# x loaded two batches ahead, gate rows issued behind the maxima, and the maxima turned earlier and sent from ScalarE

## What is computed

```
mod = silu(c) @ wmod                                   # per batch: shifts, scales and gates
h   = layernorm(x) * (1 + ca) + sa
q, k, v = h @ w_dq.T @ w_uq.T, split(h @ w_dkv.T @ w_ukv.T)   # 16 heads of 16 features
x   = x + ga * (softmax(causal(q @ k.T / 4)) @ v @ w_out.T)
h   = layernorm(x) * (1 + cb) + sb
x   = x + gb * (out0 where expert 0 has the larger logit, else out1)
      out0 = gelu(h @ W0a.T + b0a) @ W0b.T + b0b,  out1 = relu(h @ W1a.T + b1a) @ W1b.T + b1b
```

## Time and profile before

| | |
|---|---|
| median of 3 runs | 679.35 us (678.64 to 680.35) |
| the profiled execution | 680.1 us, of which the span from first to last instruction 678.3 us |
| PE busy | 560.5 us (83% of the span) |
| DVE, ACT, POOL busy | 440.7, 367.0, 267.7 us |
| mean granted TensorE clock | 0.872 of full speed |
| transfers | 43.87 MB, mean 65 GB/s |

### The profile page before, as it was taken

One profiled execution on the slowest core, in us unless ns is written; L12 is line 12 of the kernel. 1 busy time (PEld: TensorE's weight loads), 2 busy tenths in 40 slices (PEclk: granted clock), 3 DMA queues, 4 the chain that ended last, 5 costly groups with the idle time before them and its releaser, 6 DMA issues.

```text
span 678.3 us, 14114 instructions
## 1 busy us (share of the span) xinstructions
PE 560.5 (83%) x4912; PEld 472.4 (70%) x4912; DVE 440.7 (65%) x885; ACT 367.0 (54%) x521; POOL 267.7 (39%) x268
## 2 busy tenths in 40 slices
PE   5353939899797979798897979797997979799984
PEld 4242627688686868687786868686876768778874
DVE  2463436388584949586785949495876859397463
ACT  2333625747483847467473838476474748384520
POOL 3140304245252535445442525344452525253351
PEclk9755575989797989989797979899897979799997
DMA  8806070705325170807153260808062331601100
GB/s 274 151 10 95 1 128 1 125 3 77 67 51 93 23 122 2 141 0 112 29 69 73 41 101 9 132 0 138 3 88 54 57 89 32 96 1 34 33 17 15
DMA packets 43562, 43.87 MB, mean 65 GB/s; under 512 B 5360, under 2 KB 40560, under 8 KB 43520
## 3 DMA queue, kind: packets, MB, share of 16 engines
q1 hardware_dynamic: 43520, 43.33, 36.6%
HBM read 13.39 MB, written 4.23 MB: 26 GB/s over the span
## 4 chain that ended last, share of the span: by engine, by line
PE 58%; DMA 17%; SPq 14%; issue 5%; DVE 4%; ACT 2%; POOL 0%; POOLq 0%; DVEq 0%; ACTq 0%
DMA qs<-mx_rows 14%; SPq L286 11%; PE ps_t L410 7%; PE ps_t L414 6%; PE ps_s L389 6%; PE ps_o L338 4%; PE ps_c L338 4%; PE ps_o L339 4%; PE ps_o L340 4%; PE ps_c L339 3%; PE ps_c L340 3%; PE ps_a L338 3%; PE ps_a L340 3%; PE ps_a L339 2%; PE ps_o L428 2%
## 5 line engine op out<-in xcount | busy, mean ns | idle before, releaser
L803 ACT ACTIVATE score_rows<-ps_s 128x1024 f32<-128x1024 f32 x96 | 98.8, 1030 | 92.7 <-PE ps_s L389 76.6
L816 ACT ACTIVATE p<-ps_t 128x1024 f32<-128x1024 f32 x96 | 98.2, 1023 | 70.7 <-PE ps_t L414 69.8
L1225 POOL TENSOR_SCALAR_AFFINE_SELECT score_rows<-score_rows 128x512 f32<-128x512 f32 (+1 forms) x96 | 85.2, 888 | 114.8 <-ACT score_rows L803 114.7
L943 DVE TENSOR_REDUCE mx<-score_rows 128x4 f32<-128x1024 f32 (+1 forms) x96 | 115.0, 1211 | 11.0 <-POOL score_rows L1225 11.0
L410 PE MATMUL ps_t<-qs,ks 50*128 50x256 f32 (+1 forms) x512 | 60.2, 342 | 73.0 <-DMA qs<-mx_rows 72.3
L410 PEld LDWEIGHTS ps_t<-qs,ks 50*128 50x128 f32 x512 | 44.6, 229 | 82.5 <-DMA qs<-mx_rows 49.4
L389 PE MATMUL ps_s<-ks,qs 48*128 48x256 f32 (+1 forms) x512 | 58.4, 331 | 16.4 <-DMA ks<-parts_k 14.0
L866 DVE BATCH_NORM_STATS2 ln_st<-xs 128x6 f32<-128x256 f32 (+1 forms) x64 | 23.9, 414 | 73.7 <-DMA xs<-x 69.8
L1177 POOL TENSOR_TENSOR xs<-z,xs 128x512 f32<-128x512 f32 (+1 forms) x16 | 27.7, 1733 | 104.3 <-DVE z L1015 104.3
L1168 POOL TENSOR_TENSOR ln_rs<-ln_ve,neg_half 128x2 f32<-128x2 f32 x32 | 24.1, 755 | 108.7 <-DVE ln_ve L872 108.7
L389 PEld LDWEIGHTS ps_s<-ks,qs 48*128 48x128 f32 x512 | 39.8, 205 | 34.8 <-issue 21.4
(11 more groups left out here) (160 smaller groups left out, 1650.5 us busy)
## 6 DMA issues: line engine op xcount, KB each, us to landing
qs<-parts_q SPq DMA_DIRECT2D x96, 128.0 KB, 4.3
ks<-parts_k SPq DMA_DIRECT2D x96, 128.0 KB, 5.8
xs<-x SPq DMA_DIRECT2D x16, 256.0 KB, 6.7
gates<-gates_scratch SPq DMA_DIRECT2D x16, 256.0 KB, 6.1
out<-xs SPq DMA_DIRECT2D x16, 256.0 KB, 5.6
p<-wmod SPq DMA_DIRECT2D x1, 1024.0 KB, 6.2
p<-waT SPq DMA_DIRECT2D x1, 1024.0 KB, 8.3
p<-wmod SPq DMA_DIRECT2D x1, 512.0 KB, 5.9
```

The lines of the kernel that those rows point to most:

```text
L803: act.activation(score_rows[c % 2][:], ps_s[:], ACT.Copy).then_inc(scores_out, 1)
L816: act.activation(by_side, ps_t[:].rearrange("p (k h s) -> p k h s", k=2, h=n // 2), ACT.Exp, scale=SCALE).then_inc(exp_done, 1)
L943: dve.tensor_reduce(dst, score_rows[c % 2][:].rearrange("p (k h s) -> p k h s", k=2, h=n), AX_X, ALU.max).then_inc(max_done, 1)
L1225: pool.affine_select(out=diag, in_=diag, compare_op=ALU.is_ge, fill=NEG, base=0, pattern=[[0, n], [-1, P]], channel_multiplier=1).then_inc ...
```

## The change

Four things are changed. The maxima are turned in the bank of the keys (`ps_b`), and one step earlier in the listing: `turn_maxima(at(1), ...)` stands before the last `up` group of the step rather than `turn_maxima(at(2), ...)` at the head of the next. ACT itself issues the two transfers of the maxima, behind a wait for its own copy, and `maxima_rows` stands before `values_copy` instead of behind it. SP no longer issues the maxima. And SP loads x two batches ahead, as the last transfer of its step. The lists of bank users follow these moves.

```diff
-        BANK = dict(... V=ps_o, MT=ps_c, OT0=ps_o, ...
+        BANK = dict(... V=ps_o, MT=ps_b, OT0=ps_o, ...
@@ SP
-            def load_maxima(b):
-                if b.off:
-                    return
-                sp.wait_ge(mt_ready, b.n + 1)
-                for k in range(2):
-                    sp.dma_start(qs[b.parity][ODD * k + R:ODD * k + RM, :, :].bitcast(F32), mx_rows[NH * k:NH * (k + 1), :].bitcast(F32)).then_inc(maxrows_in, 16)
...
                 load_gates(at(2))
-                prefetch_x(at(-1))
-                load_maxima(at(1))
                 stack_k(at(0), 1)
                 store(at(4))
+                prefetch_x(at(-2))
@@ PE
             def step(at):
-                turn_maxima(at(2), ("UP0", at(4)), ("Q", at(1)))
                 turn_values(at(3), 0, ("PVb", at(3)))
-                turn_values(at(3), 1, ("K", at(1)), ("CKV", at(1)), ("GX", at(5)))
-                up(at(4), 2, ("MT", at(2)), ("UP0", at(4)))
+                turn_values(at(3), 1, ("MT", at(2)), ("K", at(1)), ("CKV", at(1)), ("GX", at(5)))
+                up(at(4), 2, ("UP0", at(4)))
...
                 values(at(2), 3)
+                turn_maxima(at(1), ("K", at(0)), ("CKV", at(0)), ("GX", at(4)), ("AT", at(3)), ("OT1", at(3)), ("MT", at(2)), ("K", at(1)))
                 up(at(3), 1, ("DN1", at(4)), ("T1", at(0)))
@@ ACT
                 act.activation(mx_rows[:], BANK["MT"][0:2 * NH, 0:S], ACT.Copy).then_inc(mt_ready, 1)
+
+                act.wait_ge(mt_ready, b.n + 1)
+                for k in range(2):
+                    act.dma_start(qs[b.parity][ODD * k + R:ODD * k + RM, :, :].bitcast(F32), mx_rows[NH * k:NH * (k + 1), :].bitcast(F32)
+                                  ).then_inc(maxrows_in, 16)
...
             def step(at):
                 gelu(at(4), 0)
+                maxima_rows(at(2))
                 values_copy(at(3), 1)
-                maxima_rows(at(2))
                 gelu(at(4), 1)
```

More of the change, by code:

```diff
@@ L208, in block_kernel @@
         ST_OF_GROUP = (2, 3, 5, 6)
-        BANK = dict(T1=ps_a, Q=ps_c, CKV=ps_b, K=ps_b, V=ps_o, MT=ps_c, OT0=ps_o, OT1=ps_b, AT=ps_b, OP=ps_c, T2=ps_c,
+        BANK = dict(T1=ps_a, Q=ps_c, CKV=ps_b, K=ps_b, V=ps_o, MT=ps_b, OT0=ps_o, OT1=ps_b, AT=ps_b, OP=ps_c, T2=ps_c,
                     GT=ps_a, GX=ps_b, UP0=ps_c, UP1=ps_a, UP2=ps_c, UP3=ps_o, DN0=ps_o, DN1=ps_a, PVa=ps_o, PVb=ps_o)
@@ L636, in step @@
                 up(at(4), 3, ("V", at(1)), ("OT0", at(3)), ("PVb", at(3)), ("PVa", at(3)), ("DN0", at(5)))
-                project_out(at(3), ("UP2", at(4)), ("MT", at(2)))
+                project_out(at(3), ("UP2", at(4)), ("Q", at(1)))
                 s_chunk(at(1), 0)
@@ L640, in step @@
                 turn_z1(at(0), ("GT", at(4)), ("UP1", at(4)), ("DN1", at(5)), ("T1", at(1)))
-                turn_gate(at(4), ("AT", at(3)), ("OT1", at(3)), ("K", at(1)), ("CKV", at(1)), ("GX", at(5)))
+                turn_gate(at(4), ("AT", at(3)), ("OT1", at(3)), ("MT", at(2)), ("K", at(1)), ("CKV", at(1)), ("GX", at(5)))
                 down(at(4), 0, 0, ("UP3", at(4)))
@@ L650, in step @@
                 turn_z2(at(3), ("OP", at(3)))
-                compress(at(0), ("GX", at(4)), ("AT", at(3)), ("OT1", at(3)), ("K", at(1)))
+                compress(at(0), ("GX", at(4)), ("AT", at(3)), ("OT1", at(3)), ("MT", at(2)), ("K", at(1)))
                 st_chunk(at(2), 4)
@@ L654, in step @@
                 s_chunk(at(1), 4)
-                project_q(at(0), ("T2", at(3)), ("OP", at(3)), ("UP2", at(4)), ("MT", at(2)), ("UP0", at(4)), ("Q", at(1)))
+                project_q(at(0), ("T2", at(3)), ("OP", at(3)), ("UP2", at(4)), ("UP0", at(4)), ("Q", at(1)))
                 st_chunk(at(2), 5)
```

## The result

The changed kernel takes 661.63 us (median of 4 runs, 657.57 to 662.02) against 679.85 us of the kernel before on the same chip. The ratio is 0.972, with a 95% interval of 0.968 to 0.976. It is faster, as forecast, but by 18 us rather than 66, and outside the range of 597 to 640.

What follows compares the result with a forecast made beforehand. PE's wait for late maxima bounds the kernel. Waits 54.7 plus clock 33.8, less new waits 22.1, plus filling 7, less last batch 1.5, save 71.9 us; clock falls return 5.2: 613.4, as median 612.6 us, range 597 to 640.

Steps and rivals of the forecast that it cites:

- What bounds the kernel: PE at `st_chunk` 0 idles 4.4 us for late maxima and loses 2.6 us by the clock, 7.0 us per steady step.
- The maxima's landing: Maxima issued by ACT at 315.9 and 316.6 land at about 321, so the wait at `st_chunk` 0 is gone.
- the upper bound: Maxima landing as long after issue as now, 6.9 us, so at 323.6, leaving 1.6 us of wait at `st_chunk` 0.
- Rival B: Maxima still land behind everything SP has in flight; 1.6 us of wait stay in 13 steps; about 636 us, chance 0.15.
- ACT's two transfers: Issuing the pair takes ACT 1.4 us and delays `values_copy`, so PE newly waits 1.5 us for its values.
- Turning ahead at nothing: Starting `turn_maxima` at 314.62, just after `k_low` leaves the keys' bank, costs nothing; the cover is 0.1 us.
- SP's list: The last two k stacks reach `s_chunk` 0 with 1.6 us margin, nothing added; x a step early costed at nothing.
- The clock: Full clock gives 2.6 us in each of 13 steps, 33.8 us; falls in 2 of them take back 5.2 us.
- The filling steps: Last k stacks take over as the wait; 1.5 of the first 8.18 us and 5.5 of the second 9.4 gained, 7 together.

Runs made afterwards that it cites:

- SP ahead of the keys: SP issues the maxima ahead of all k stacks: from the changed kernel 644.64 and, gate rows last, 617.04 us; from the kernel before 728.55 and, x two batches ahead, 670.05 us.
- keys held: Changed kernel, with SP waiting for ACT's copy of the maxima before issuing any k stack, and x ahead of that wait: 618.18 us, ratio 0.908.
- pair split, keys behind: Changed kernel, with ACT issuing one maxima transfer and SP the other at the same time, then k stacks, gate rows, store and x: 607.35 us, ratio 0.894.

## Why the prediction was wrong

**What bounds the kernel**: right. The maxima behind a full line of transfers, 4.4 us of idleness and 2.6 us of clock per step.

**The maxima's landing**: this is the step that failed. I put it at 321 between bounds of 319.2 and 323.6, by a transfer of ACT sharing the engines with SP's stacks instead of standing behind them. It landed at 324.6 in the same count, 1.0 us beyond the upper bound. ACT's transfer had to let pass nearly all that SP had issued before it, the gate rows too: its first packet comes 5.4 us after its issue. My own rows had the gate rows going out at 315.95, beside ACT's first issue at 315.9, and yet I left them out of what is ahead.
The upper bound was right as a mechanism and missed one thing, for which the prediction also had the figure: it put the k stacks at 316.4, between ACT's issues at 315.9 and 316.6. SP does issue a k stack at 342.02, between ACT's two issues, and the second transfer lands 1.6 us behind the first. x was taken out of the line and k stacks came in.
(The prediction says that the second transfer is issued by 317.79. That is where its issue starts; the pair of 1.40 us is issued by 318.45. The sum is not touched, since both the 6.87 us and the bound count from the start of the second issue.)

From the first issue of the pair to its landing, in batches 4 to 12:

| | us |
|---|---|
| before | 7.0 to 7.6 |
| changed kernel | 7.5 to 8.9 |
| SP ahead of the keys, in the four kernels that do so | 2.9 to 3.0 |
| keys held, ACT issues | 4.7 to 6.2 |
| pair split, keys behind | 2.6 to 3.4 |

The run with the keys held shows that this step, with the clock that hangs on it, separates the forecast from the result: with the landing early, a step takes 32.5 to 33.0 us, against 32.5 in the forecast, and the time is 618.18 us against 612.6.
The Trainium skill ("DMA: Bandwidth & Descriptors", Queues, rings and completion order) has each engine taking packets in turn from the issuers' queues. The trace agrees only from the moment at which ACT's packets appear: the 16 packets of its first transfer stand between 346.93 and 347.24, among 95 of SP's. For the 5.4 us before that no turn was given to it. What the Trainium skill states on the same page under "Issuing engines are not separate DMA queues" agrees with the runs as far as that ACT's issuing makes no transfer faster; its word that a second issuer saves issue time is what the split pair used, with both issues at 347.40.

**Rival B** had the mechanism, at 636 us. It kept 1.6 us of wait per step where 2.6 were kept, mostly since it missed the k stack, and it took few falls of the clock, where more than half of the steps had a stretch at 0.50 like those shown.

**ACT's two transfers**: right. 1.28 us for the pair and 1.47 us of wait at `turn_values`, against 1.4 and 1.5.

**Turning ahead at nothing**: right in a steady step, no row of PE waiting for `k_low` there. The thin cover did show in the filling, where PE waits for it twice, 5.0 us in total, with 3.8 the longest. And in the changed kernel the turning seems to have brought nothing in a steady step, since the landing was set by the line; no run takes it back alone.

**SP's list**: right that the k stacks do not bind. x was undervalued. Its move is worth some 11 us alone (by the landing), and loading it two batches ahead is what lets x stand last at all: one batch ahead in that place costs 58 us where the maxima go ahead of the keys.

**The clock**: I took two falls in 13 steps at 2.6 us. In the changed kernel there are six in ten steps, at 1.7 us each. With the keys held there are none in the middle; the other fast kernels have up to four.

**The filling steps**: not separated by an experiment. From the first `st_chunk` 0 to the third, the profiled run takes 65.1 us where the one before took 71.9: 6.8 less, near the 7 of the forecast. But the first one came 6.0 us later, at 70.66 against 64.64. Some 4 us of that are there already when PE comes to its first `turn_maxima`, and the first `st_chunk` 0 of the other runs varies by more, from 61.9 to 69.1. So how much of the 6.0 is the change's doing stays open.

## What to carry to other kernels

If a small transfer that an engine waits for is issued while bulk transfers are in flight, moving it to another issuer or issuing it 1 us earlier changed little here; what helped was to hold back the bulk that nothing needs yet, so that the small one is ahead of it in time. Then look at what the held transfers feed, since the wait moves there (here `s_chunk` 0, and DVE at x), and move what is needed last to the end of the list, loaded one step earlier if its place is then too late. An idle time cut in two pieces can be worth more than its length, if the long piece costs the clock.

## What was not expected of the hardware

- A transfer of ACT waited for what SP had issued before it. ACT issued its pair from 341.52, between SP's gate rows at 341.48 and its next k stack at 342.02. In the records of single packets, the first one of ACT's queue is at 346.93, 5.4 us after the issue, when the last packets of the gate rows are moved; from there on its packets stand mixed with those of that k stack. The second transfer's begin at 348.17. In the nine steps from the issue at 269.40 to the one at 559.84 the first packet took 5.3 to 5.6 us; with the keys held it took 1.3 to 1.9.
- The length of a wait alone does not tell whether the clock falls. A wait of 1.1 to 1.6 us in every step left the granted clock at 1.00 for 494.9 us on end, while two waits of 1.5 and 2.6 us with 4 us of work between them cost it in six steps of ten, for 3.4 us each. And with SP issuing the maxima and the gate rows behind the keys, it fell for 3.4 us in three steps of the middle, each time within 2.2 us behind the start of the matmul that ended a wait of only 1.1 to 1.2 us. What tells these cases apart no run here shows.
